# A graph layer with residual layernorm: a circular order of blocks and rounds, and one chunk before the loop of pairs

## The chip, the cores and the metric

The kernel runs on one core of a Trainium2 chip. The metric is the time of the kernel on the device in microseconds; the median of three timed runs before the change is 714.42 us (713.59 to 715.35).

## The reference

There are 100,000 nodes with 64 features (x), and 50,000 edges with 32 features each (edge_attr), a source and a destination node. The edges come sorted by destination, and destinations are drawn as 100000 * u^2 with u uniform, so they crowd at the low nodes.

```python
msg = jnp.concatenate([x[row], edge_attr], axis=1) @ W1 + b1      # 96 -> 128
agg = jax.ops.segment_sum(msg, col, num_segments=x.shape[0])
y = x + jnp.concatenate([x, agg], axis=1) @ W2 + b2               # 192 -> 64
out = (y - mean(y)) / sqrt(var(y) + 1e-5)                         # per node, over 64 features
```

## The kernel before

**Algebra.** W1 is multiplied with the part of W2 that meets agg, so an edge needs only z = [x[src], edge_attr, 1] @ wz with 64 columns. The mean over features is taken out of the weights (wz, wx, b2), and the residual is put into wx, so that what is left of the layernorm is a root and a product.

**Edges.** They are cut into chunks of 128 (392 places, CHUNKS), taken in the descending order, from the edges of the last nodes to those of node 0. Eight chunks are an edge round, 49 rounds in all (PAIRS). GpSimd gathers the rows of x for a round by eight indirect DMAs (`gather`, L381) into one of two halves of two buffers (feat), ScalarE's queue loads edge_attr beside them (L560). TensorE transposes (`turn`, L409) and multiplies with wz (`message`, L417). z is kept as three bf16 parts whose sum is the fp32 value: ScalarE makes the high part (`z_highs`, L578) and the middle (`z_mids`, L584), VectorE the rest after the high part (`z_rests`, L725) and the low part (`z_lows`, L792). All of z stays in SBUF.

**Nodes.** 1024 nodes are a block (98 of them), 256 a group (4 in a block), two blocks a unit (49 units, `unit`). For each block VectorE makes one-hots from the chunks' destinations (`one_hots`, L806) and copies z's window of these chunks (L809); TensorE multiplies one with the other into ps_y (`block_sum`, L490, 12 matmuls a group for two chunks), and adds x @ wx (L468 transposes x, L481 multiplies) and the bias (L477). ScalarE squares with a sum (L596), keeps y (L600), takes the root (L608), VectorE the reciprocal (L837) and the product (L842, for the unit before); SyncE's queue loads x and stores out.

**How many chunks.** A group of 256 nodes may have its edges in 1 to 20 chunks. The first two are always taken. If any group of a block has more (register `second`), all four groups take a second pair, in the same buffers, once TensorE has summed the first (`group_summed`). If any group still has more (`third`), each such group runs a loop over further pairs (L830 one-hots into onehot_x, L521 matmuls straight from z; one buffer for each of the pair's two chunks, given back by `hotx_used`).

**What sets the order.** At the start the kernel finds with VectorE for each group its first and last chunk (L729 to L739), makes from them the steps of each block (steps) and, for each round, how many units may have run (units: all blocks whose chunks are there, but at most AHEAD = 2.125 blocks a round), and brings both through DRAM into one row, from which the engines read registers. Loop round k of TensorE, ScalarE and VectorE does edge round k (or the steps of rounds just before it) and then the units that index k - LAG of the table adds (LAG = 2). The last indices (46 to 49 on TensorE) are unrolled copies of the unit's code behind the loop, each skipped by a branch where it has no unit. At index 49 all remaining units run.

## Time and profile before

| | us |
|---|---|
| median of the timed runs | 714.42 |
| profiled execution | 712.24 |
| its span, first to last instruction | 710.3 |
| TensorE matmul busy | 566.6 (80%) |
| VectorE busy | 519.7 (73%) |
| GpSimd busy | 398.9 (56%) |
| ScalarE busy | 397.4 (56%) |
| mean granted TensorE clock (1 is full) | 0.907 |

Busy counts instructions that compute or move; loads of registers, branches and semaphore steps are not in it, and where an engine stands idle for them the profile writes "issue". L numbers are lines of the kernel before. A row of a timeline merges like instructions: start, length, engine, line, what is written from what, how many, and in brackets the idle time just before and what ended it.

### The profile page before, as it was taken

To read this page: it belongs to the slowest core of one execution; us is meant where nothing else is said; L and a number is where in the kernel's file an instruction comes from. 1 tells how busy PE (TensorE), PEld (TensorE's weight loads), DVE (VectorE), ACT (ScalarE), POOL (GpSimd) and SP (SyncE) were. 2 spreads that over 40 slices of the span, in tenths; PEclk is the share of its full clock that TensorE was granted. 3 is DMA by queue.
4 is the path that set the end of the run, shared out by engine and by line. 5 is a ranking of instruction groups with operands and counts; after the bars stand their busy time and mean duration, and the time that the engine had idled before them with its cause. 6 is when DMAs were issued, how large, how long until landed. Compare 5 with 4: busy or idle time off the path is not lost. (4 is left out here: it accounts for less than half of the span.)

```text
span 710.3 us, 28935 instructions
## 1 busy us (share of the span) xinstructions
PE 566.6 (80%) x8370; PEld 507.2 (71%) x8371; DVE 519.7 (73%) x1820; ACT 397.4 (56%) x2012; POOL 398.9 (56%) x418
## 2 busy tenths in 40 slices
PE   1365798998888888898889888898888888873774
PEld 1355687888777877787778878787777777763653
DVE  2684677778788877778778778778888888863443
ACT  0011478777777777777777777776544445532101
POOL 5777657777757777766774777765744444000000
PEclk9955799999999999999999999999999999985555
DMA  2122345545545555545555545554433333220002
GB/s 63 33 38 38 81 123 147 136 120 132 147 117 149 127 124 138 141 122 126 142 136 136 133 120 131 139 132 114 99 83 81 81 81 96 81 59 7 2 1 60
DMA packets 168746, 71.33 MB, mean 100 GB/s; under 512 B 61570, under 2 KB 162447, under 8 KB 168720
## 3 DMA queue, kind: packets, MB, share of 16 engines
q1 hardware_dynamic: 104592, 51.74, 25.5%
q0 software_dynamic: 12544, 12.87, 9.8%
q10 hardware_dynamic: 51584, 6.41, 5.8%
q8 instruction: 13, 0.21, 0.1%
q14 instruction: 13, 0.11, 0.1%
HBM read 45.37 MB, written 25.60 MB: 100 GB/s over the span
## 5 line engine op out<-in xcount | busy, mean ns | idle before, releaser
L381 POOL DMA_INDIRECT feat<-in_x,src_idx x392 | 391.9, 1000 | 197.9 <-issue 117.7
L806 DVE TENSOR_SCALAR onehot<-node_of_col,group_base,dst_of 128x256 bf16<-128x256 bf16 x944 | 288.0, 349 | 90.8 <-issue 81.2
L490 PEld LDWEIGHTS ps_y<-z_window,onehot 128*128 128x128 bf16 x5664 | 195.1, 100 | 48.8 <-DVE z_window L809 30.2
L490 PE MATMUL ps_y<-z_window,onehot 128*128 128x64 bf16 x5664 | 213.5, 196 | 18.0 <-DVE z_window L809 14.1
L596 ACT ACTIVATE square<-ps_y 128x64 bf16<-128x64 f32 x784 | 162.1, 238 | 94.7 <-PE ps_y L481 91.9
L596 ACT ACTIVATION_READ_ACCUMULATOR square<-ps_y 128x1 f32 x784 | 159.1, 224 | 0.0
L417 PE MATMUL ps_z<-wz,feat_t 97*128 97x64 f32 x784 | 106.0, 293 | 31.5 <-DVE z_rest L725 31.4
L481 PE MATMUL ps_y<-wx,x_t 128*128 128x128 f32 x784 | 114.9, 291 | 18.5 <-ACT x_t L589 12.7
L417 PEld LDWEIGHTS ps_z<-wz,feat_t 97*128 97x128 f32 x784 | 100.3, 207 | 40.3 <-DVE z_rest L725 36.5
L809 DVE COPY z_window<-z 128x384 bf16 x472 | 121.6, 258 | 0.0
L481 PEld LDWEIGHTS ps_y<-wx,x_t 128*128 128x128 f32 x784 | 99.1, 197 | 22.3 <-ACT x_t L589 16.5
L556 ACT ACTIVATE feat_t<-ps_t 97x512 f32<-97x512 f32 x98 | 58.5, 597 | 98.2 <-PE ps_z L417 78.9
L600 ACT ACTIVATE y_sb<-ps_y 128x512 f32<-128x512 f32 x98 | 61.4, 626 | 76.6 <-DVE yout L842 76.6
L409 PE MATMUL ps_t<-ident,feat 128*97 128x128 f32 x392 | 59.7, 297 | 33.5 <-DMA feat<-in_x,src_idx 18.2
L409 PEld LDWEIGHTS ps_t<-ident,feat 128*97 128x97 f32 x392 | 48.4, 176 | 42.7 <-issue 24.6
L842 DVE TENSOR_TENSOR yout<-y_sb,rstd 128x512 f32<-128x512 f32 x100 | 64.7, 688 | 1.7
L468 PE MATMUL ps_x<-ident,xin 128*128 128x128 f32 x392 | 56.3, 291 | 8.4 <-issue 8.4
L792 DVE TENSOR_TENSOR z<-z_rest,z 128x512 f32 (+1 forms) x49 | 33.9, 692 | 38.0 <-ACT z L584 22.2
L589 ACT ACTIVATE x_t<-ps_x 128x512 f32<-128x512 f32 x98 | 53.5, 600 | 6.9 <-PE ps_x L468 6.7
L468 PEld LDWEIGHTS ps_x<-ident,xin 128*128 128x128 f32 x392 | 48.6, 156 | 9.0 <-issue 9.0
L725 DVE TENSOR_TENSOR z_rest<-ps_z,z 128x512 f32<-128x512 f32 x49 | 33.9, 691 | 13.3 <-DVE z L792 11.8
L578 ACT ACTIVATE z<-ps_z 128x512 f32 (+1 forms) x49 | 29.2, 597 | 23.7 <-issue 17.9
(113 smaller groups left out, 214.3 us busy)
## 6 DMA issues: line engine op xcount, KB each, us to landing
xin<-in_x SPq DMA_DIRECT2D x97, 256.0 KB
out<-yout SPq DMA_DIRECT2D x97, 256.0 KB
feat<-in_x,src_idx POOLq DMA_INDIRECT x392
feat<-in_edge_attr ACTq DMA_DIRECT2D x96, 64.0 KB
z<-in_src SPq DMA_DIRECT2D x1, 192.0 KB
z<-in_dst SPq DMA_DIRECT2D x1, 192.0 KB
xin<-in_x SPq DMA_DIRECT2D x1, 128.0 KB
out<-yout SPq DMA_DIRECT2D x1, 128.0 KB
```

The costliest lines, as they stand in the source:

```text
L381: nc.gpsimd.indirect_dma_start(out=feat[h][:, feat_at(k) + feat_slot(c), 0:C], out_offset=None, in_=x[:, :], in_offset=bass.IndirectOffset ...
L409: tr = nc.tensor.transpose(ps_t[h][0:F, c * P:(c + 1) * P], feat[h][:, half * CB + feat_slot(c), :], ident[:, :])
L417: mm = nc.tensor.matmul(ps_z[:, (h * CB + c) * C:(h * CB + c + 1) * C], feat_t[h][:, c * P:(c + 1) * P], wz[:, :], start=True, stop=True)
L468: tr = nc.tensor.transpose(ps_x[h][:, g * P:(g + 1) * P], xin[h][:, g, :], ident[:, :])
L481: return nc.tensor.matmul(ps_y[h][:, g * A * C:(g + 1) * A * C], x_t[h][:, g * P:(g + 1) * P], wx[:, :], start=False, stop=(g == G - 1))
L490: mm = nc.tensor.matmul(ps_y[h][:, col:col + C], onehot[h][:, g, s, a, :], z_window[h][:, g, s, part * C:(part + 1) * C], start=False, sto ...
L556: nc.scalar.activation(feat_t[h][:, :], ps_t[h][0:F, :], ACT.Copy).then_inc(feat_ready[h], 1)
L596: sq = nc.scalar.activation(square[h][:, q, :], ps_y[h][:, q * C:(q + 1) * C], ACT.Square, accum_out=sumsq[:, h, q:q + 1])
L600: nc.scalar.activation(y_sb[h][:, :, :], ps_y[h][:, :].rearrange("p (n c) -> p n c", c=C), ACT.Copy).then_inc(y_kept[h], 1)
L806: ins = nc.vector.tensor_scalar(onehot[h][:, g, s, :, :], node_of_col[:, :, :], base, dst_of[:, bass.ds(firsts[g] + (at + s), 1)], ALU.add ...
L809: nc.vector.tensor_copy(z_window[h][:, g, :, :], z[:, bass.ds(firsts[g] + at, 2), :, :].rearrange("p s q c -> p s (q c)")).then_inc(window, 1)
L842: nc.vector.tensor_tensor(yout[h][:, :, :], y_sb[h][:, :, :], rstd[:, h, :].rearrange("p (n o) -> p n o", o=1).to_broadcast([P, G * A, C]) ...
```

## The change

The edges are no longer reversed. Rounds start at round 24 (chunk 192) and go up to the end, wrap to chunk 0 and end at chunk 191 (`chunk_at`); blocks start at block 25, go up to 97, wrap to 0 and end at 24. Unit 36 holds block 97, the cut one, and block 0. Chunk numbers in the table stay plain, and `need` is brought into the circular order by a few more short steps. The last batch of edges is three chunks that end with the last edge, and destinations that stand twice are set to -1, so there is no part of a chunk to load. ScalarE's loop over rounds is split in two by four unrolled rounds around the turn (TURN = 25, rounds 23 to 26), VectorE's by one (27); SyncE's queue gets two loops, too.

The second change is in the steps. If any group of a block has more than two chunks, all groups take one chunk in the window buffers (before: two), and what is beyond three goes through the loop in pairs, ceil((n-3)/2) of them for a group with n chunks (before: ceil((n-4)/2)).

```diff
+FIRST_BLOCK = 25
+FIRST_ROUND = 24
+FIRST_CHUNK = 2 * CB * FIRST_ROUND
+CUT_UNIT = (BLOCKS - 1 - FIRST_BLOCK) // 2
+TURN = PAIRS - FIRST_ROUND
...
+        def chunk_at(k, turned=False):
+
+            if isinstance(k, int):
+                return 2 * CB * ((k + FIRST_ROUND) % PAIRS)
+            return 2 * CB * k + (FIRST_CHUNK - (CHUNKS if turned else 0))
...
-                    pair_sum(g).then_inc(group_summed, 1)
+                    window_sum(g, 2).then_inc(group_summed, 1)
                 with pe.If(second > 0):
...
-                        pair_sum(g)
+                        window_sum(g, 1)
...
-                                                                      z[:, chunk + (4 + s), part, :], start=False, stop=False)
+                                                                      z[:, chunk + (3 + s), part, :], start=False, stop=False)
...
+            with act.Fori(LAG + 2, TURN - 2) as k:
+                act_round(k)
+            for k in range(TURN - 2, TURN + 2):
+                act_round(k)
+            with act.Fori(TURN + 2, PAIRS - 1) as k:
+                act_round(k, turned=True)
...
-            nc.vector.tensor_copy(src_idx[:, 0:LAST_CHUNK + 1], ps_t[0][:, LAST_CHUNK::-1])
-            nc.vector.tensor_copy(src_idx[:, LAST_CHUNK + 1:CHUNKS], ps_t[0][:, LAST_CHUNK + 1:CHUNKS])
-            nc.vector.tensor_copy(dst_of[:, 0:LAST_CHUNK + 1], ps_t[1][:, LAST_CHUNK::-1])
-            nc.vector.tensor_copy(dst_of[:, LAST_CHUNK + 1:CHUNKS], ps_t[1][:, LAST_CHUNK + 1:CHUNKS]).then_inc(s_idx, 1)
-            dve.wait_ge(s_idx, 1)
+            nc.vector.tensor_copy(dst_of[:, :], ps_t[1][:, 0:CHUNKS]).then_inc(s_dve, 1)
+            nc.vector.tensor_copy(src_idx[:, :], ps_t[0][:, 0:CHUNKS]).then_inc(s_idx, 1)
...
+            link(nc.vector.tensor_scalar(last[:, :], last[:, :], -1.0, None, ALU.add))
             link(nc.vector.tensor_scalar(need[:, :], first[:, :], 3.0, None, ALU.add))
             link(nc.vector.tensor_tensor(need[:, :], need[:, :], last[:, :], ALU.max))
+            link(nc.vector.tensor_scalar(far_first[:, :], first[:, :], float(FIRST_CHUNK), float(CHUNKS - 1), ALU.is_lt, ALU.mult))
+            link(nc.vector.scalar_tensor_tensor(out=far_first[:, :], in0=need[:, :], scalar=float(FIRST_CHUNK),
+                                                in1=far_first[:, :], op0=ALU.is_ge, op1=ALU.mult))
+            link(nc.vector.tensor_scalar(wrapped[:, :], need[:, :], float(FIRST_CHUNK), float(CHUNKS), ALU.is_lt, ALU.mult))
+            link(nc.vector.scalar_tensor_tensor(out=need[:, :], in0=need[:, :], scalar=float(-FIRST_CHUNK),
+                                                in1=wrapped[:, :], op0=ALU.add, op1=ALU.add))
+            link(nc.vector.tensor_tensor(need[:, :], need[:, :], far_first[:, :], ALU.max))
...
-                for g in range(G):
-                    pair(g, 0, hot_ready, window_ready)
+                for g in range(G):
+                    window_of(g, 0, 2, hot_ready, window_ready)
                 with dve.If(second > 0):
                     for g in range(G):
                         dve.wait_ge(group_summed, G * b + g + 1)
-                        pair(g, 2, hot2_ready, window2_ready)
+                        window_of(g, 2, 1, hot2_ready, window2_ready)
...
-            with dve.Fori(LAG + 2, PAIRS + 1) as k:
+            with dve.Fori(LAG + 2, TURN + 2) as k:
                 dve_round(k)
+            dve_round(TURN + 2)
+            with dve.Fori(TURN + 3, PAIRS + 1) as k:
+                dve_round(k, turned=True)
```

`window_sum(g, chunks)` and `window_of(g, at, chunks, hot, window)` are `pair_sum` and `pair` with the number of chunks as an argument in place of 2. SyncE's loads and stores follow the new order; at the cut unit the load of the part of block 97 waits for the one before it.

## Rows read from the trace of the kernel before

**Rows 1.** Table of stages: the middle, and the pair loops of the last block
```profile
core 0: us, PE busy (x) PEld busy (x) DVE busy (x) ACT busy (x) POOL busy (x), PEclk, DMA share, GB/s
...
281.40:379.20 97.80, 87.28 (x1294) 79.44 (x1292) 76.80 (x262) 71.73 (x360) 71.52 (x71) 0.97 0.54 133
679.70:701.00 21.30, 14.62 (x168) 11.38 (x168) 9.20 (x28) 0.00 (x0) 0.00 (x0) 0.53 0.00 0
```
**Rows 2.** Waits of VectorE from 300 to 400 us: total, times, longest
```profile
DVE onehot L806 <- issue: 15.4, 19, 1.0
DVE z L792 <- issue: 3.2, 9, 0.4
DVE z_rest L725 <- DVE z L792: 2.0, 8, 0.3
```
**Rows 3.** Timeline of VectorE: starts of two plain rounds, and one with two units
```profile
111.74 0.69 DVE L792 TENSOR_TENSOR z<-z_rest,z 128x512 f32 x1 [0.37 <-issue]
...
122.61 0.69 DVE L792 TENSOR_TENSOR z<-z_rest,z 128x512 f32 x1 [0.36 <-issue]
...
378.88 0.24 DVE L837 RECIPROCAL rstd<-std 128x16 f32<-128x16 f32 x1
...
387.09 0.25 DVE L837 RECIPROCAL rstd<-std 128x16 f32<-128x16 f32 x1
```
**Rows 4.** Timeline of VectorE: a round whose blocks both take a second pair
```profile
503.27 0.69 DVE L792 TENSOR_TENSOR z<-z_rest,z 128x512 f32 x1 [0.35 <-issue]
...
510.01 0.59 DVE L806 TENSOR_SCALAR onehot<-node_of_col,group_base,dst_of 128x256 bf16<-128x256 bf16 x2
510.53 0.25 DVE L809 COPY z_window<-z 128x384 bf16 x1
510.70 0.59 DVE L806 TENSOR_SCALAR onehot<-node_of_col,group_base,dst_of 128x256 bf16<-128x256 bf16 x2
...
519.62 0.69 DVE L792 TENSOR_TENSOR z<-z_rest,z 128x512 f32 x1 [0.35 <-issue]
```
**Rows 5.** Timeline of VectorE: end of unit 47, and unit 48
```profile
631.19 1.29 DVE L842 TENSOR_TENSOR yout<-y_sb,rstd 128x512 f32<-128x512 f32 x2
...
654.40 0.60 DVE L806 TENSOR_SCALAR onehot<-node_of_col,group_base,dst_of 128x256 bf16<-128x256 bf16 x2 [2.01 <-issue]
...
660.17 0.60 DVE L806 TENSOR_SCALAR onehot<-node_of_col,group_base,dst_of 128x256 bf16<-128x256 bf16 x2 [2.96 <-PE ps_y L490]
...
677.48 0.26 DVE L809 COPY z_window<-z 128x384 bf16 x1
...
681.09 0.35 DVE L830 TENSOR_SCALAR onehot_x<-node_of_col,group_base,dst_of 128x256 bf16<-128x256 bf16 x1 [2.28 <-PE ps_y L521]
...
684.19 0.65 DVE L830 TENSOR_SCALAR onehot_x<-node_of_col,group_base,dst_of 128x256 bf16<-128x256 bf16 x2 [0.83 <-PE ps_y L521]
685.67 0.65 DVE L830 TENSOR_SCALAR onehot_x<-node_of_col,group_base,dst_of 128x256 bf16<-128x256 bf16 x2 [0.83 <-PE ps_y L521]
```
**Rows 6.** Timeline of TensorE: stalls in its first unit and in its last
```profile
78.38 1.05 PE L481 MATMUL ps_y<-wx,x_t 128*128 128x128 f32 x8 [2.41 <-issue]
...
83.39 2.07 PE L481 MATMUL ps_y<-wx,x_t 128*128 128x128 f32 x8 [2.35 <-issue]
...
655.27 0.87 PE L468 MATMUL ps_x<-ident,xin 128*128 128x128 f32 x3 [6.93 <-issue]
...
680.29 1.14 PE L521 MATMUL ps_y<-z,onehot_x 128*128 x12 [1.84 <-issue]
```
**Rows 7.** Groups by line: all one-hots for the windows and for the loop
```profile
L806 DVE TENSOR_SCALAR onehot<-node_of_col,group_base,dst_of 128x256 bf16<-128x256 bf16 x944 | 288.0, 349 | 90.8 <-issue 81.2 <-PE ps_y L481 6.0 <-PE ps_y L490 3.6
L830 DVE TENSOR_SCALAR onehot_x<-node_of_col,group_base,dst_of 128x256 bf16<-128x256 bf16 x38 | 12.2, 346 | 18.1 <-PE ps_y L521 16.5 <-issue 1.5
```
**Rows 8.** Timeline of GpSimd: gathers of the first rounds
```profile
74.50 1.26 POOL L381 DMA_INDIRECT feat<-in_x,src_idx  x1 [0.30 <-issue]
...
84.95 1.00 POOL L381 DMA_INDIRECT feat<-in_x,src_idx  x1 [0.30 <-issue]
...
93.83 0.97 POOL L381 DMA_INDIRECT feat<-in_x,src_idx  x1 [7.88 <-PE ps_t L409]
```

More of the change, by code:

```diff
@@ L27 @@
 CHUNKS = BATCHES * CB
-FULL_CHUNKS = E // P
-LAST_CHUNK = -(-E // P) - 1
-E_TAIL = E - FULL_CHUNKS * P
+BATCH_EDGES = CB * P
+LAST_EDGES = E - (CB - 1) * P
+TWICE = (BATCHES - 1) * BATCH_EDGES - LAST_EDGES
 A = 2
@@ L301, in store, with store_round, load_round @@
                 sp.dma_start(dst_ap, yout[h][:, :, :].rearrange("p (g a) c -> p g (a c)", g=G)).then_inc(out_stored[h], 16)
[L303 to L304 removed]
+            def store_round(k, at, cut=0):
                 for h in range(2):
[L306 removed]
+                    free_yout(k, h, cut)
                 for h in range(2):
[L308 removed]
+                    store(k, h, out_blocks[2 * k + at + h])
             for h in range(2):
                 sp.sem_inc(yout_free[h])
[L312 to L318 removed]
+            def load_round(k, at):
+                for h in range(2):
+                    load_x(k, h, x_blocks[2 * k + at + h])
+            low, high = FIRST_BLOCK, FIRST_BLOCK - BLOCKS
+            load_round(1, low)
+            load_round(2, low)
+            store_round(0, low)
+            with sp.Fori(2, CUT_UNIT - 1) as k:
+                load_round(k + 1, low)
+                store_round(k - 1, low)
+            sp.wait_ge(x_used[0], CUT_UNIT)
+            whole, cut = tail_parts(x)
+            sp.dma_start(xin[0][0:TAIL_PARTS, TAIL_GROUPS, :], cut).then_inc(x_cut_loaded, 16)
+            load_x(CUT_UNIT, 1, x_blocks[0])
+            sp.wait_ge(x_cut_loaded, 16)
+            sp.dma_start(xin[0][:, 0:TAIL_GROUPS, :], whole).then_inc(x_loaded[0], 16)
+            store_round(CUT_UNIT - 2, low)
+            load_round(CUT_UNIT + 1, high)
+            store_round(CUT_UNIT - 1, low)
+            load_round(CUT_UNIT + 2, high)
+            for h in range(2):
+                free_yout(CUT_UNIT, h)
+            sp.wait_ge(out_ready[0], CUT_UNIT + 2)
             whole, cut = tail_parts(out)
@@ L322, in _ @@
             sp.dma_start(cut, yt[0:TAIL_PARTS, TAIL_GROUPS, :]).then_inc(out_stored[0], 16)
-            store(0, 1, out_block(1))
-            with sp.Fori(2, PAIRS - 1) as k:
-                top = sp.snap(BLOCKS - 2 * k)
-                for h in range(2):
-                    load_x(k + 1, h, x_full[top - (3 + h)])
-                store_round(k - 1, top + 1)
-            store_round(PAIRS - 2)
-            store_round(PAIRS - 1)
+            store(CUT_UNIT, 1, out_blocks[0])
+            with sp.Fori(CUT_UNIT + 2, PAIRS - 1) as k:
+                load_round(k + 1, high)
+                store_round(k - 1, high, cut=1)
+            store_round(PAIRS - 2, high, cut=1)
+            store_round(PAIRS - 1, high, cut=1)
             sp.wait_ge(out_stored[0], 16 * (PAIRS + 1))
@@ L482, in dense, with window_sum @@
                                             wx[:, :], start=False, stop=(g == G - 1))
-                def pair_sum(g):
-                    for s in range(2):
+                def window_sum(g, chunks):
+                    for s in range(chunks):
                         for a in range(A):
@@ L621, in _ @@
                 act.sem_inc(squared[h])
-            act.wait_ge(s_clear, 8)
-            load_ea_first()
-            load_ea(0, 1)
-            act.wait_ge(s_const, 13)
+            act.wait_ge(s_clear, 7)
+            for h in range(2):
+                load_ea(0, h)
+            act.wait_ge(s_const, 14)
             nc.scalar.activation(std_eps[:, :], eps[:, :], ACT.Sqrt)
@@ L801, in one_hots, with window_of @@
                 dve.wait_ge(hots_used[h], k + 1)
-                def pair(g, at, hot, window):
+                def window_of(g, at, chunks, hot, window):
                     base = group_base[:, bass.ds(b * G + g, 1)]
-                    for s in range(2):
+                    for s in range(chunks):
                         ins = nc.vector.tensor_scalar(onehot[h][:, g, s, :, :], node_of_col[:, :, :], base,
@@ L826, in one_hots @@
                                     turn_no = dve.snap(pairs_done)
-                                    chunk = nc.s_assert_within(dve.snap(firsts[g] + 2 * n), 0, CHUNKS - 6, skip_runtime_bounds_check_because="the table of steps ends every range before the last chunk")
+                                    chunk = nc.s_assert_within(dve.snap(firsts[g] + 2 * n), 0, CHUNKS - 5, skip_runtime_bounds_check_because="the table of steps ends every range before the last chunk")
                                     for s in range(2):
```

172 lines of the change are left out of this document (76 added, 96 removed).

## The prediction

> **What bounds the kernel now.** I read the table of stages first: in the long middle TensorE is busy 87.28 of 97.80 us and VectorE 76.80 [rows 1], which reads like a TensorE bound. The waits of VectorE in that stage say otherwise: from 300 to 400 us it waited for "issue" (its own sequencer: loops and register loads) and for a short step behind itself, and for no other engine [rows 2]. So its own chain of instructions sets the pace. The timeline of VectorE prices that chain: a round (eight chunks of edges, one unit of two blocks) starts at 111.74 and the next at 122.61, 10.87 us; where a round runs two units, reciprocals stand 387.09 - 378.88 = 8.2 us apart [rows 3]. So a unit costs 8.2 us of VectorE and the bare round 2.66. The rounds of blocks with a second pair take 519.62 - 503.27 = 16.35 us [rows 4], 5.5 more than a plain round: per block 4 groups, each 0.68 (two one-hots 0.52, one copy 0.17, by the starts 510.01, 510.53, 510.70), 2.74 per block. The same sum from 122.61 us (loop round 8, five units done) gives 40 x 2.66 + 43 x 8.2 + 18 x 2.74 = 508.3, so 630.9 for the end of unit 47; the trace has 631.19 + 1.29 [rows 5]. The account holds to 1 us.
>
> Behind it lies the tail. VectorE ends unit 47 at 632.5 and starts the one-hots of unit 48 at 654.40, 22 us later: the last three edge rounds go through all engines with no unit beside them, and TensorE waits 6.93 us for issue before its next x transpose [rows 6]. Unit 48 (blocks 1 and 0) then takes until the end at 710.3.
>
> **Counts.** The trace fixes those of before: 944 one-hots are 392 x 2 + 20 x 8, so 20 blocks take the second pair, and 38 one-hots of L830 are 19 pairs in the loop [rows 7]. From the reference's dst, sorted into chunks of 128, I get the same 20 and 19 (1, 4 and 14 in blocks 2, 1, 0), and so trust it for after: 21 blocks take the third chunk (97, 0 to 18 and 20), and 31 pairs are in the loop (18, 5, 4, 2, 1, 1 in blocks 0 to 5). The table of units for each round comes from the same data. Before: 2, 1, 1, 1, 1 ... from index 2 on, 48 units by index 45, the last one at index 49. After: 0, 1, 1, 2, 1, 1, 1, 2 for indices 2 to 9 (9 units either way by then), one a round to index 37 (39 units), then 7 units over indices 38 to 48 and three (46, 47, 48) at index 49; of those three only one block takes a third chunk.
>
> **Part 1, one chunk in place of a pair.** Of the 2.74 us a block, one one-hot (0.26) stays of each two. The copy of 128x192 has no row. It lies between the 0.17 of 128x384 and half of that, 0.09 [rows 4]. I take the middle, 0.13: 4 x 0.39 = 1.56 a block, 21 blocks 32.8 us against 20 x 2.74 = 54.8. Gain 22.0 (20 to 23.5). TensorE's 456 fewer window matmuls (960 before, 21 x 24 after) save nothing of their own there, since it waits for VectorE's windows in those rounds.
>
> **Part 2, more pairs in the loop.** Block 0 before: last window copy 677.48 + 0.25, the second pair's one-hot at 681.09, so 3.36 us to get in, most of it TensorE loading its registers (1.84 issue [rows 6]) while VectorE waits; then 685.67 - 684.19 = 1.48 a pair, one-hots and matmuls taking turns through one buffer each [rows 5]. On VectorE before: block 0 22.5, block 1 7.3, block 2 0.7, together 30.5. After: 4 blocks x 3.36 = 13.4, 25 further pairs x 1.48 = 37.0, and blocks 4 and 5 with one pair and no wait 1.3 each: 53.0. Loss 22.5. The 1.48 has the 12 matmuls at the half clock (granted 0.53 there [rows 1]), 1.04 us of it. At the full clock they would take half, so 1.48 - 0.26 (half of one buffer's six) = about 1.2: lower end 22.5 - 7 = 15. Upper end, 1.8 a pair with the switches of groups (block 1's 7.3 over 4): 30.
>
> **Part 3, the circular order at the start.** Before, index 2 has two units at once. After, the first block needs 14 chunks, so index 2 has none, and VectorE idles behind the gathers: POOL needs 84.95 - 74.50 = 10.45 us for eight [rows 8], and before TensorE has units these set the pace. Gathers of round 5 end at 75.8, its transposes at about 77, those of rounds 6 and 7 follow about 10.4 apart. The first unit on TensorE costs twice a warm one (two stalls of 2.4 for issue, and the half clock; before it ended at 83.39 + 2.07 [rows 6]): it ends at about 96. Then unit 1 and the two of index 5 follow, and VectorE starts round 8 at about 120 with 4 units done; before it was 122.61 with 5. Loss 8.2 - 2.6 = 5.6 (3 to 9). The ten or so extra short steps in making the tables (0.2 us each) lie beside the wait for those gathers: nothing; uncovered they would be 2. Dropping the reversed copies saves VectorE four column copies, also hidden.
>
> **Part 4, the circular order at the end.** Idle of VectorE before: 21.9 between 632.5 and 654.4, less three rounds of its own work (8.0), 13.9; and 2.96 for TensorE at 660.17 [rows 5]. After, units 44 and 45 lie between the last rounds. What is left: ScalarE makes the middle part of round 47 only after the high part of round 48, which waits for TensorE's message behind unit 44 (3.7 us of VectorE idle), and about 1.2 for one-hot buffers in the last units. Gain 16.9 - 4.9 = 12.0 (6 to 15). From the last one-hot to the end it is 10.1 before and as much after: dense matmuls, squares, root, product, store.
>
> TensorE's first pass through unrolled units is the doubt here. The tail has one copy of the unit's code for each of indices 46, 48 and 49, where before only that of 49 ran. Twice 2.4 per copy [rows 6] lies partly in the 1 to 2 us a unit by which TensorE is ahead. The Trainium skill, page "Runtime: NRT & Kernel Launch", section "Instruction fetch mechanics", says that a taken branch to a page outside the current window must fetch before going on. If each skipped section and skipped copy stalled so with nothing to hide it, the eight such jumps of the tail at 2.4 would be 19 us, and the gain of this part gone. The rows show such stalls in the first unit and in the tail, and none at the like places of the loop once it is warm, which agrees.
>
> **Part 5, what the middle pays.** (a) The pair loops now stand before warm rounds. In the pair loops before, the clock was at its lower level nearly throughout (0.53 [rows 1]), after TensorE had worked in bursts of 1.04 in 1.48 us. After it, TensorE starts blocks 1 to 6 at half speed, where its 9.7 us a round (87.28/97.80 of 10.87) goes towards 19 against VectorE's 14 to 30: 5 us until it has caught up (0 to 12). (b) ScalarE runs four rounds and VectorE one from unrolled copies near the turn, with new loops behind: VectorE's first window in such a copy was late by 1 us (2.01 issue [rows 5] against 1.0 at most in the loop [rows 2]); with the tail 4 us in all (0 to 8). Skewed x loads at the cut block, two DMAs one behind the other, lie beside a unit of 8 us: nothing. Edge, x and output transfers keep their number and sizes.
>
> **Sum.** -22.0 + 22.5 + 5.6 - 12.0 + 5 + 4 = +3.1 us on the span of 710.3: 713.4. The profiled execution took 712.24 (1.9 around its span), the median of the timed ones is 714.42, 2.2 above it. So 714.42 + 3.1 = 717.5.
>
> **Rivals.** *A, the pair loop and the cold code are cheap.* In mid-stream the clock stays at its upper level (it is 0.97 in the middle [rows 1]), a pair costs 1.2, nobody meets cold code: -22.0 + 15.5 + 5.6 - 14 + 0 + 1 = -14, so 700. For it: VectorE alone waited only for issue at its first entry into the loop. Against: in a pair loop TensorE has at most 0.53 of 1.2 us to do, less than where the clock fell before. In part (3 or more us kept of these) the kernel is already faster, about 709.
> *B, TensorE becomes the bound.* The clock stays down through units 36 to 40 and the three cold copies of the tail are exposed: +3.1 + 7 + 9 = +19, so 733 (727 to 736 with less or more of it). For it: the half clock after 679.7 us never recovered while pair loops ran. Against: plain units fill TensorE densely, and hold the clock at 0.97 in the middle [rows 1].
> *C, the rounds without a unit are bound by the gathers.* Indices 38, 40, 43 and 47 run no unit; at 10.45 us of POOL instead of 2.66 four of them would cost 31, so 748. POOL runs up to two rounds ahead and waited 7.88 us for TensorE [rows 8]; the units between last 14 us and more, so I count it as small.
> *D, the new order of blocks and rounds is made but the tail keeps its wait*, since three units still have to follow the last chunk: +3.1 + 12 = 729, inside B's place.
>
> **Chances.** The near cancellation 0.48 (its own range 712 to 724), A 0.26, B and D 0.22, C 0.04. Within 0.3% (2.1 us, about what can be told from no change) is the lower third of the first case: 0.17. Faster: A and the lowest edge of the first, 0.33. Slower: 0.50. Range 701 to 732: it holds nearly all of A and the nearer half of B.
>
> **What would show it.** L806 x868 one-hots, L809's line x476 copies, L830's line x62, TensorE's window matmuls 4704 + 504 = 5208. Rounds of about 14 us with third chunks; block 0's stretch of VectorE near 500 us, 25 to 30 us long; no idle of 8 us in VectorE's last 80 us; loop round 8 at 120. I am wrong if the pair loops run at the full clock, if TensorE's waits for VectorE vanish in the second half, or if POOL gathers until the end.

## The result: slower by 4.15%

The changed kernel took 743.62 us median of 4 runs (742.46 to 745.17), the kernel before beside it 714.00 (713.09 to 715.35): a ratio of 1.0415, 95% interval [1.0388, 1.0441]. I had forecast 717.5, from 701 to 732. The profiled execution took 742.46, with a span of 740.6 against 710.3.

The page's groups by line (columns: line, engine, operation, tiles, count | busy us, mean ns of one | idle before and what ended it), which answer to [rows 7], and the stages that answer to [rows 1]:

```profile
L831 DVE TENSOR_SCALAR onehot<-node_of_col,group_base,dst_of 128x256 bf16<-128x256 bf16 x868 | 268.0, 350 | 107.0 <-issue 89.6
...
L509 PE MATMUL ps_y<-z_window,onehot 128*128 128x64 bf16 x5208 | 205.0, 198 | 21.8 <-DVE z_window L834 17.7
...
L834 DVE COPY z_window<-z 128x384 bf16 (+1 forms) x476 | 117.9, 248 | 0.0
```

```profile
core 0: us, PE busy (x) PEld busy (x) DVE busy (x) ACT busy (x) POOL busy (x), PEclk, DMA share, GB/s
281.40:379.20 97.80, 87.02 (x1316) 78.15 (x1314) 76.77 (x261) 72.57 (x369) 74.30 (x72) 1.00 0.53 132
476.00:502.00 26.00, 17.75 (x204) 13.76 (x204) 11.01 (x34) 0.00 (x0) 0.00 (x0) 0.56 0.00 0
```

The counts are those forecast (868, 476, 5208), so the kernel does what it says. The middle is as before, 76.77 against 76.80 us of VectorE. The pair loops of block 0 now run in mid-stream, from 476 on, at the same low clock (0.56 against 0.53).

To see where the 30 us came from, I followed VectorE's starts of a round (the first tensor_tensor on z of each loop index; the list of starts is worked out from its timeline). Both kernels have finished 36 units when they start round 37: before at 454.3, after at 461.6, 7.3 later. From there to the end it is 256.0 and 279.0, 23.0 more. Rounds 37 to 50, us each:

```
round   37    38    39    40    41    42    43    44    45    46    47    48    49    50
before 10.9  10.8  13.6  13.6  16.3  17.7  16.4  16.3  16.4  29.6  16.8  10.1   6.7   2.1
after  42.5  30.8  22.3   8.2  22.2   6.0  18.0  16.2   6.0  18.3  14.6  16.3   6.7  14.0
```

Rounds 40, 42 and 45 after run no unit. I had counted such a round at VectorE's own 2.66 us. VectorE's timeline of the kernel after, for the first two of them and the block behind the first (start, length, ..., idle before and what ended it):

```profile
558.09 0.69 DVE L734 TENSOR_TENSOR z_rest<-ps_z,z 128x512 f32<-128x512 f32 x1 [0.26 <-DVE z L817]
565.32 0.69 DVE L817 TENSOR_TENSOR z<-z_rest,z 128x512 f32 x1 [6.54 <-ACT z L596]
...
573.61 0.35 DVE L831 TENSOR_SCALAR onehot<-node_of_col,group_base,dst_of 128x256 bf16<-128x256 bf16 x1 [3.12 <-PE ps_y L509]
...
593.49 0.69 DVE L817 TENSOR_TENSOR z<-z_rest,z 128x512 f32 x1 [4.32 <-ACT z L596]
```

VectorE stands 6.54 and 4.32 us for ScalarE's middle part of z, and, between the two, 3.12 us in round 41's first block, ahead of its third chunk, for TensorE's sums of the first two chunks, since that chunk goes through the same window buffer. VectorE's waits from round 37 to the end, after:

```profile
DVE onehot L831 <- issue: 31.7, 29, 2.8
DVE onehot_x L855 <- PE ps_y L540: 24.5, 25, 2.2
DVE z L817 <- ACT z L596: 20.2, 4, 6.5
DVE onehot L831 <- PE ps_y L509: 13.6, 16, 3.2
```

and before, from its round 37 to its end:

```profile
DVE onehot L806 <- issue: 23.6, 27, 2.0
DVE onehot_x L830 <- PE ps_y L521: 16.5, 16, 2.3
DVE z L792 <- ACT z L584: 14.1, 3, 8.4
...
DVE onehot L806 <- PE ps_y L490: 3.6, 2, 3.0
```

The wait for ScalarE, which my part 4 took to be mostly gone, grew from 14.1 to 20.2; that for TensorE's window sums went from 3.6 to 13.6; the pair loops' from 16.5 to 24.5.

### The profile page after: what moved, and what is told of

Read it like the earlier page. It is cut to its first block and busy times, and to the rows that moved or that the text cites. A ratio compares the mean times of both kernels' runs of the same rounds, so it can differ in the third digit from the quotient of the medians.

```text
span 740.6 us, 27987 instructions
## 1 busy us (share of the span) xinstructions
PE 591.2 (80%) x8058; PEld 524.3 (71%) x8059; DVE 507.3 (69%) x1777; ACT 399.4 (54%) x2012; POOL 399.0 (54%) x418
## 3 DMA queue, kind: packets, MB, share of 16 engines
q1 hardware_dynamic: 104592, 51.74, 24.5%
## 5 line engine op out<-in xcount | busy, mean ns | idle before, releaser
L403 POOL DMA_INDIRECT feat<-in_x,src_idx x392 | 392.9, 1002 | 249.4 <-PE ps_t L428 122.9
L831 DVE TENSOR_SCALAR onehot<-node_of_col,group_base,dst_of 128x256 bf16<-128x256 bf16 x868 | 268.0, 350 | 107.0 <-issue 89.6
L509 PEld LDWEIGHTS ps_y<-z_window,onehot 128*128 128x128 bf16 x5208 | 185.9, 101 | 56.2 <-DVE z_window L834 32.8
L509 PE MATMUL ps_y<-z_window,onehot 128*128 128x64 bf16 x5208 | 205.0, 198 | 21.8 <-DVE z_window L834 17.7
L436 PE MATMUL ps_z<-wz,feat_t 97*128 97x64 f32 x784 | 112.5, 305 | 26.6 <-DVE z_rest L734 26.4
L436 PEld LDWEIGHTS ps_z<-wz,feat_t 97*128 97x128 f32 x784 | 106.9, 219 | 37.2 <-DVE z_rest L734 33.5
L834 DVE COPY z_window<-z 128x384 bf16 (+1 forms) x476 | 117.9, 248 | 0.0
L428 PE MATMUL ps_t<-ident,feat 128*97 128x128 f32 x392 | 65.6, 316 | 39.3 <-DMA feat<-in_x,src_idx 17.4
L428 PEld LDWEIGHTS ps_t<-ident,feat 128*97 128x97 f32 x392 | 54.0, 192 | 48.2 <-issue 22.8
L487 PE MATMUL ps_x<-ident,xin 128*128 128x128 f32 x392 | 58.8, 300 | 1.7 <-issue 1.7
L540 PE MATMUL ps_y<-z,onehot_x 128*128 x372 | 32.1, 227 | 24.4 <-DVE onehot_x L855 18.3
L540 PEld LDWEIGHTS ps_y<-z,onehot_x 128*128 128x128 bf16 x372 | 24.6, 112 | 31.8 <-issue 28.8
## 6 DMA issues: line engine op xcount, KB each, us to landing
xin<-in_x SPq DMA_DIRECT2D x97, 256.0 KB
out<-yout SPq DMA_DIRECT2D x97, 256.0 KB
```

The costliest lines, as they stand in the source:

```text
L403: nc.gpsimd.indirect_dma_start(out=feat[h][:, feat_at(k) + c, 0:C], out_offset=None, in_=x[:, :], in_offset=bass.IndirectOffsetOnAxis(ap=s ...
L428: tr = nc.tensor.transpose(ps_t[h][0:F, c * P:(c + 1) * P], feat[h][:, half * CB + c, :], ident[:, :])
L436: mm = nc.tensor.matmul(ps_z[:, (h * CB + c) * C:(h * CB + c + 1) * C], feat_t[h][:, c * P:(c + 1) * P], wz[:, :], start=True, stop=True)
L487: tr = nc.tensor.transpose(ps_x[h][:, g * P:(g + 1) * P], xin[h][:, g, :], ident[:, :])
L509: mm = nc.tensor.matmul(ps_y[h][:, col:col + C], onehot[h][:, g, s, a, :], z_window[h][:, g, s, part * C:(part + 1) * C], start=False, sto ...
L831: ins = nc.vector.tensor_scalar(onehot[h][:, g, s, :, :], node_of_col[:, :, :], base, dst_of[:, bass.ds(firsts[g] + (at + s), 1)], ALU.add ...
```

## Experiments

In every kernel below but desc_even and desc_even2 the first unit's number of a round passes through a max with zero (the register is never negative, so this changes no work). The kernels ran in five groups (the expectations say "call" for a group), each on one chip and beside the kernel before. In groups 1 and 4 that took 712.97 and 712.38 us, in groups 2, 3 and 5 it took 1067.88, 1068.70 and 1070.08 (the slow groups below). So times compare within a group only; where I set kernels of two groups side by side below, I take each less the kernel before of its own group.

**Group 1: the two parts of the change apart.** The control circ_c is the changed kernel with that max. circ_two has the circular order with the second pair of before; desc_one has the order of before with one chunk in place of the second pair (both edits in short, side by side):

```
 circ_two (against after)                 desc_one (against before)
-window_of(g, 2, 1, ...)                 -for s in range(2): onehot of 2 + s
+window_of(g, 2, 2, ...)                 +for s in range(1)
-chunks beyond three in the loop         -chunks beyond four in the loop (19 pairs)
+chunks beyond four (19 pairs)           +chunks beyond three (31 pairs)
```

> The changed kernel with one more register step per round on each engine: the number of units already done goes through a max with 0 before it starts the loop of units. Nothing else differs. It is the control for the kernels beside it, which all carry this step. One step of 0.1 us or less in about 45 rounds, beside other work: 743 to 747, against 743.6 of the changed kernel.

> The circular order with the steps of before: a second pair for all groups of a block (21 blocks, 20 plus the one with block 97), and only then pairs in the loop, 19 as before in place of 31. Theory E: the two kinds of steps cost the same within 3 us (2.74 against 1.56 us a block is +22, twelve pairs at 1.48 and three entries fewer is -22), so 740 to 747. Theory P: the pair loops in mid-stream are what costs; with twelve fewer, and none in blocks 3 to 5, it is 10 us or more faster than the control, 733 or less. Theory O (the single one-hot catches up with TensorE: VectorE waited 13.6 us in 16 waits for the sum of the first pair before it wrote the third chunk): these waits go, 730 to 736.

> The descending order of before with the second change alone: one chunk for all groups of 20 blocks, then 31 pairs in the loop in place of 19. My sum for this part was -22.0 and +22.5: 712 to 717. Theories P and O, by which this part carries the loss: 725 or more. Theory E, by which the order carries it: within 4 us of 714.

circ_c: 745.79, ratio 1.0445 [1.0386, 1.0505]. circ_two: 738.07, 1.0354 [1.0313, 1.0394]. desc_one: 719.09, 1.0103 [1.0055, 1.0152]. The chunk costs 6.1 us alone (desc_one less before) and 7.7 in the circular order. The order costs 25.1 (circ_two less before) or 26.7 (circ_c less desc_one). The two add up, and four fifths of the loss is the order. Neither of these two times lies in a range that I had written down. 738.07 stands midway between theory O's 736 and theory E's 740; but VectorE's waits for TensorE's sums, which O said would go, are 16.0 us in its trace. 719.09 is 1 to 2 us above the upper ends of my sum and of theory E, and 6 below P and O. Rounds with two third-chunk blocks last 14.7 in desc_one against 16.35 in [rows 4]: 0.8 a block saved, where I had 1.18. One-hot and copy of the one chunk are 0.38 us apart by their starts, as I had it (0.39); the 0.7 us by which a round is longer than my 13.98 lies between the blocks, as issue: 1.06 and 1.43 us ahead of the two blocks of round 41, where before had 0.98 and 0.75 in the round of [rows 4]. Over the whole stretch from round 37 VectorE's waits for issue before a window are 30.5 us in desc_one and 23.6 in before, 6.9 more, which is about the chunk's price of 6.1. What VectorE's sequencer does in them isn't shown.

**Group 1: one unit for each index.** circ_even is circ_c with another table of units, so that no index is without one from 3 to 48:

```
-AHEAD = 2.125
+AHEAD = 2.0
-nc.gpsimd.iota(round_no[:, :], pattern=[[0, 1]], base=0,
+nc.gpsimd.iota(round_no[:, :], pattern=[[0, 1]], base=-2,
```

> The changed kernel with another table of units: at most 2 * (k - 2) blocks by index k, in place of 2.125 * k. By the reference's dst this gives one unit for every index from 3 to 48 and three at index 49, so no round without a unit (before: indices 38, 40, 43, 47) and none with two. Theory E (rounds without a unit): in loop rounds 40, 42 and 45 the chain transpose, feat_t, message, high, rest, middle, low passes the engines with nothing beside it (8.2, 6.0 and 6.0 us where VectorE has 2.66 of work), and the unit behind starts with TensorE late (16 to 22 us where the account has 14 to 15.3). Then 15 to 25 us come back: 720 to 729. Theory P (the pair loops and TensorE at its half clock behind them): the table changes neither, within 4 us of the control.

It took 727.66 us (720.55 to 731.79), ratio 1.0176 [1.0110, 1.0241], 18.1 less than circ_c and within theory E's 720 to 729; its runs spread over 11 us, so the 18.1 is good to some 6 us either way. VectorE's waits from its round 37 to the end (in the execution of 731.79) have no row for ScalarE's z at all:

```profile
...
DVE onehot L839 <- PE ps_y L517: 14.4, 22, 5.0
...
DVE z L825 <- issue: 4.4, 13, 0.4
DVE rstd L870 <- ACT std L628: 4.2, 1, 4.2
DVE z_rest L742 <- DVE z L825: 3.4, 13, 0.3
```

So the rounds without a unit are a large part of the loss. The waits for TensorE's sums stay (14.4, in 22 waits). 11.2 of them lie between 550 and 602 us, in the two rounds with the last four pairs, in which the granted clock was 0.63 and 0.61; that the clock makes them is likely and not tested.

**Group 4: both orders without any pair loop.** circ_nopairs3 and desc_one_nopairs3 leave the chunks beyond the third out of the sums, by a table that says zero pairs; the same two had run in groups 2 and 3 as circ_nopairs, circ_nopairs2, desc_one_nopairs and desc_one_nopairs2. circ_c2 is the control again.

```
-link(nc.vector.reduce_sum(far_first[:, 1:2], pairs_f[:, :], axis=AX.X))
+link(nc.vector.tensor_scalar(far_first[:, 1:2], block_need[:, :], 0.0, None, ALU.mult))
```

> The circular control without any pair loop (the chunks beyond the third are left out of the sums). Theory 1 (the 31 passes and the entries to their blocks cost 1.5 us and 3.5 us): 45 us less than circ_c2 of this call. Theory 2 (0.73 us a pass, as in my sum): 25 us less.

> The descending order with one chunk beyond two, without any pair loop (the chunks beyond the third are left out). Against circ_nopairs3 it differs in the order alone. Theory 1 (the rounds without a unit cost 6 us each): 12 to 20 us faster than circ_nopairs3 where VectorE bounds the plain rounds, and equal where TensorE does. Theory 2 (the order costs only through its pair loops): within 5 us in both cases.

> The control (the changed kernel, with the first unit's number held at zero or more) beside the kernels of this call. If the chip is like that of the first call: a ratio of 1.044 as there. If it is like that of the second and third, where each plain round is bound by TensorE: theory 1 (the order's rounds without a unit and the pair loops are longer than VectorE's own work whatever TensorE does) a ratio of 1.01 to 1.03, theory 2 (there the order costs nothing, since the loop's rounds are TensorE's) 0.99 to 1.00.

circ_c2: 745.31, ratio 1.0449 [1.0405, 1.0494], as in group 1. circ_nopairs3: 686.32 (682.51 to 691.22), 0.9627 [0.9561, 0.9693]. desc_one_nopairs3: 659.70 (658.82 to 660.59), 0.9258 [0.9222, 0.9293]. Two prices follow. The loops cost 59.0 us in the circular order (circ_c2 less circ_nopairs3), and 58.8 in that of before (desc_one of group 1 and desc_one_nopairs3, each less its own before), so where they stand makes no difference. And the order costs 26.6 us with no loop in either kernel, the same as with them. Both are more than theory 1 had (45 and 12 to 20), and far from theory 2 (25 and under 5). The two times, 686.32 and 659.70, lie in the ranges that I had set from the rounds of the traces for circ_nopairs and desc_one_nopairs (678 to 687, 658 to 666). The order's price has nothing to do with where it puts the loops.

What the price is shows in VectorE's waits from round 37 to the end, circ_nopairs3 first:

```profile
DVE onehot L839 <- issue: 30.7, 28, 2.6
DVE z L825 <- ACT z L604: 18.0, 4, 5.0
DVE onehot L839 <- PE ps_y L517: 12.4, 11, 3.1
DVE z L825 <- issue: 3.4, 10, 0.4
...
DVE rstd L870 <- ACT std L628: 2.7, 1, 2.7
```

and desc_one_nopairs3:

```profile
DVE onehot L812 <- issue: 30.4, 26, 2.1
DVE z L798 <- ACT z L592: 9.6, 2, 5.0
DVE z L798 <- issue: 5.8, 13, 1.9
DVE rstd L843 <- ACT std L616: 4.0, 1, 4.0
...
DVE onehot L812 <- PE ps_y L498: 1.6, 4, 1.1
```

That is 8.4 more for ScalarE's z and 10.8 more for TensorE's sums, 15.8 in all with the smaller rows; from round 37 to the end the two kernels differ by 222.0 - 203.5 = 18.5. The other 10.1 of their spans (685.5 and 656.9) has been lost by round 37. The descending order has rounds without a unit too, 48, 49 and 50 (6.2, 6.7 and 3.3 us), so the 18.5 is the difference of two kernels that both pay for such rounds. The chain inside round 40 of circ_nopairs3, over three engines (VectorE's, TensorE's and ScalarE's timelines):

```profile
509.06 0.69 DVE L825 TENSOR_TENSOR z<-z_rest,z 128x512 f32 x1 [0.34 <-issue]
510.00 0.69 DVE L742 TENSOR_TENSOR z_rest<-ps_z,z 128x512 f32<-128x512 f32 x1 [0.26 <-DVE z L825]
515.02 0.69 DVE L825 TENSOR_TENSOR z<-z_rest,z 128x512 f32 x1 [4.32 <-ACT z L604]
...
523.31 0.34 DVE L839 TENSOR_SCALAR onehot<-node_of_col,group_base,dst_of 128x256 bf16<-128x256 bf16 x1 [3.04 <-PE ps_y L517]
```

```profile
510.75 2.00 PE L444 MATMUL ps_z<-wz,feat_t 97*128 97x64 f32 x16 [0.93 <-DVE z_rest L742]
514.37 2.45 PE L436 MATMUL ps_t<-ident,feat 128*97 128x128 f32 x8 [1.62 <-DMA feat<-in_edge_attr]
516.71 3.68 PE L444 MATMUL ps_z<-wz,feat_t 97*128 97x64 f32 x16
...
522.31 2.69 PE L517 MATMUL ps_y<-z_window,onehot 128*128 128x64 bf16 x66
```

```profile
511.95 0.60 ACT L583 ACTIVATE feat_t<-ps_t 97x512 f32<-97x512 f32 x1 [0.77 <-PE ps_z L444]
...
513.62 0.60 ACT L598 ACTIVATE z<-ps_z 128x512 f32 x1 [0.18 <-issue]
514.12 0.62 ACT L604 ACTIVATE z<-z_rest 128x512 f32 x1
```

Read it in this order: VectorE's rest (510.00) frees the one PSUM tile of messages; TensorE then multiplies for 2.00 us; ScalarE, which has waited for those matmuls to copy the transposed features, writes the high part at 513.62 and the middle part at 514.12; VectorE's low part follows at 515.02 and the round is over, 5.96 us after 509.06, when it began. No engine works through it, they take turns (of the 5 us from 509 on TensorE is busy 2.82, VectorE 1.38, and ScalarE 3.75, 2.2 of that still for the unit before). Beside a unit of 8 us this chain is hidden; alone it is the round. One link of it is the program's own: ScalarE's middle part needs only VectorE's rest, which was there at 510.69, but `act_round` has it behind the high part of the next round, which needs TensorE's products. No run moved it ahead.

Then TensorE waits 1.62 for edge_attr, and its transposes and products take 2.45 and 3.68 us where those just before took 1.09 and 2.00: the granted clock was 1.00 from 509 to 512 and 0.50 from 513 to 523, and fell behind the wait of 0.93 and within that of 1.62. So its first window sums end past 523, and VectorE's third chunk waits 3.04. That is read from the timeline: no run took the edge_attr wait or the low clock away here, so how they share the 3.04 isn't shown. The round behind lasts 17.8 instead of 14.7. An empty round costs 6.0 - 2.66 + 3.1 = 6.4 us above my count, three of them 19, about what circ_even gave back (18.1).

In groups 2 and 3, where TensorE bounds the plain rounds (in circ_nopairs it is busy 105.88 and waits 53.2 for issue of the 160 us from 300 on), these two kernels took 1016.31 and 1018.45, then 1018.67 and 1016.64 us: equal. Taken for an answer on the order, that would have been theory 2's; group 4 shows that it held only for such runs.

> The control circ_c without the loop of pairs: the register that lets a block into it is 0 for all blocks, so all that lies beyond a group's third chunk (blocks 0 to 5) is left out of the sum. All else runs. My account had 53 us for the 31 pairs, which would give 692. From the trace of the changed kernel the rounds 37, 38, 39 and 41 took 117.8 us, where a round with two third chunks and no pair took 14.6 (round 47), so 59 goes there, and TensorE no longer falls to its lower clock: rounds 40, 42 and 43 lose another 5. 678 to 687.

> The same work left out of desc_one (descending order, one chunk, 31 pairs there). Rounds 46 and 47 had 32.8 and 28.2 us and should have 26.7 and 14.7, and the last unit loses 28.5 for block 0 and 9.3 for block 1: 57 us, 719 to 662 (658 to 666). If the pairs were dearer in mid-stream than in the tail (theory P), less than 50 comes back here and over 60 in the circular order; if the order's loss lies in the rounds without a unit and in the tail (theory E), the two differences agree within 5 us.

> The circular control without any pair loop (the chunks beyond the third of every group are left out of the sums; the number of pairs is written as zero), with the kernels of this call on one chip. Theory 1 (the 31 passes of the pair loops cost what the trace after shows, 1.48 us a pass at half TensorE clock and about 3.5 us of VectorE for each block that enters a loop at all, with waits for TensorE's group sums behind them): about 45 us less than the control's 745.8, a ratio to before of 0.98, and the rounds 37, 38, 39 last about 17, 17 and 15 instead of 42.5, 30.8 and 22.3. Theory 2 (the loops cost VectorE's own 0.73 us a pass, as my sum has it, and the loss lies in the order): about 25 us less, a ratio of 1.01. Both: the rounds without a unit (40, 42, 45) stay at 6 us.

> The descending order with one chunk beyond two, without any pair loop (the chunks beyond the third are left out). Against circ_nopairs2 it differs in the order alone, with no pair in either. Theory 1 (the order's own price is that of its three rounds without a unit, 6 us each where a unit's round has room for one): 12 to 20 us faster than circ_nopairs2, a ratio to before of 0.95 to 0.96. Theory 2 (the order costs only by where it puts the pair loops, at half clock): within 5 us of circ_nopairs2.

**Groups 3 and 5: the edge_attr load issued first.** circ_ea (and circ_ea3) moves ScalarE's load of the next batch ahead of its copies.

```
 for h in range(2):
-    keep_feat(k, h)
-    load_ea(k + 1, h, turned)
+    act.wait_ge(ea_loaded[h], 16 * (k + 1))
+    load_ea(k + 1, h, turned)
+for h in range(2):
+    keep_feat(k, h)
```

> The circular control with ScalarE's load of the next edge_attr batch issued ahead of the copies of the transposed features, not behind them. Theory 1 (a round without a unit lasts 6 us because TensorE waits in it for a load that ScalarE has issued late, 1.5 us a half): the rounds 40, 42 and 45 last about 4.5 instead of 6.0 to 8.2, and the time is 5 us less than the control's, a ratio of 1.037. Theory 2 (such a round is a chain of transposes, copies, products and rests over three engines, and the load is beside it): within 1.5 us of the control, a ratio of 1.043 to 1.047.

> The circular control with ScalarE's loads of the next edge_attr batch issued ahead of its copies of the transposed features. Theory 1 (a round without a unit is 6 us long for that late load): rounds 40, 42 and 45 last about 4.5 us, a ratio of 1.037. Theory 2 (the chain of transposes, copies, products and rests is what it lasts): 1.043 to 1.047.

1077.08 (1.0077 [1.0040, 1.0113]) and 1077.24 (1.0061 [1.0038, 1.0085]), in the slow groups, without the control circ_c beside them, so the time says little. The empty rounds say more: 8.7, 7.4 and 7.6 us in circ_ea3, against 7.5, 7.6 and 6.5 in circ_busy3 of the same group, which has the loads where they were (and fillers in its pair loops, so it is no clean control). They got no shorter, which speaks for theory 2, the load beside the chain. Where the kernel before takes 712 us it wasn't measured, so whether an earlier load would save some of the 3 us behind an empty round stays open.

**Groups 2, 3 and 5: filler matmuls at the loops.** circ_busy (circ_busy2, circ_busy3) keeps TensorE at work to hold its clock.

```
 with pe.If(third > 0):
+    fill(12)
 ...
+        fill(2)
         pe.wait_ge(hotx_ready[s], done)
```

> The control circ_c with matmuls that compute nothing needed, into a PSUM bank of their own, where TensorE stands idle about the pair loops: 12 of 128x256 bf16 before a block's registers are loaded and 2 before each chunk of a pair. If TensorE's lower clock is what makes the pair loops and the rounds behind them slow, the granted clock goes from about 0.7 to near 1 from 465 to 600 us, a pair from 1.48 to 1.2, and VectorE's waits for TensorE's sums (3 to 5 us in the rounds behind) go: 725 to 735. If the entry and the pair are bound by register loads and the round trip, the filling only adds to it: 745 to 755.

> The circular control with filler matmuls on TensorE ahead of each block's pair loop (12) and in each pass (2), to a PSUM tile that nothing reads. Theory 1 (the half clock behind TensorE's waits makes a pass of a loop 1.48 us instead of VectorE's own 0.73): the granted clock in the first stretch of loops rises from half to full, a pass lasts 0.9 to 1.1, and the time is 8 to 12 us less than the control's, a ratio of 1.03. Theory 2 (a pass is a chain between VectorE and TensorE, its waits and issue gaps, whatever the clock): a pass lasts 1.4 or more, and the time is that of the control or up to 5 us over it, a ratio of 1.045 to 1.05.

> The circular control with filler matmuls on TensorE ahead of each block's pair loop (12) and in each pass (2). Theory 1 (half clock makes a pass long): a pass in the first block with loops lasts 0.9 to 1.1 us instead of 1.48, and the time is 8 to 15 us less than the control's 745.3, a ratio of 1.025 to 1.035. Theory 2 (a pass is a chain of VectorE, its issue gaps and TensorE's answer): 1.4 us a pass or more, a ratio of 1.044 to 1.055.

1070.58, 1072.77 and 1073.12 us, ratios 1.0040 [1.0022, 1.0059], 1.0036 [1.0009, 1.0063] and 1.0025 [1.0007, 1.0044]. The stretch of block 0's loops, circ_busy2 and then circ_ea3, whose TensorE has no fillers (columns as above):

```profile
745.00:775.00 30.00, 25.57 (x348) 19.25 (x347) 15.00 (x57) 1.75 (x16) 0.00 (x0) 0.91 0.00 0
```

```profile
760.00:775.00 15.00, 10.63 (x122) 8.31 (x122) 6.58 (x21) 0.00 (x0) 0.00 (x0) 0.50 0.00 0
```

One pass with fillers, VectorE and TensorE:

```profile
766.15 0.65 DVE L871 TENSOR_SCALAR onehot_x<-node_of_col,group_base,dst_of 128x256 bf16<-128x256 bf16 x2 [0.79 <-PE ps_y L556]
767.59 0.65 DVE L871 TENSOR_SCALAR onehot_x<-node_of_col,group_base,dst_of 128x256 bf16<-128x256 bf16 x2 [0.79 <-PE ps_y L556]
```

```profile
766.54 0.39 PE L524 MATMUL ps_idle<-node_of_col 128*128 128x256 bf16 x2 [0.24 <-issue]
766.77 0.58 PE L556 MATMUL ps_y<-z,onehot_x 128*128 x6
767.18 0.38 PE L524 MATMUL ps_idle<-node_of_col 128*128 128x256 bf16 x2
767.40 0.34 PE L556 MATMUL ps_y<-z,onehot_x 128*128 x6
```

The clock rose from 0.50 to 0.91, and a pass still takes 1.44 us against 1.48: my forecast of 0.9 to 1.1 failed. But the four fillers of a pass lie in TensorE's row between the real matmuls (0.22 us each two, by the starts) and take back what the clock gave, so this doesn't tell what a pass would last at the full clock alone. It stays open. In the times of group 4 the fillers weren't measured.

**Groups 2 and 4: one unit for each index in the order of before.** desc_even and desc_even2 are the kernel before with AHEAD = 2.0, nothing else.

> The kernel before (descending order, second pairs) with at most 2.0 blocks a round in place of 2.125, so that units 44 to 47 run at indices 45 to 48 beside the last edge rounds, where before there was none. Before, VectorE had 8 us of work in the 21.9 between its last two units. Theory E: most of the 13.9 comes back, 700 to 706. If a tail without units costs nothing (the last unit sets the end anyway): 712 to 715.

> The kernel before with 2.0 instead of 2.125 indices for a block, so that each index has one unit: no round of two units. Theory 1 (two units in a round cost no more than two rounds, and what counts is the number of units left behind the last index): 0 to 6 us faster, a ratio of 0.992 to 1.0. Theory 2 (one unit fewer in the tail is paid by one more far-window unit in the loop at the same price): 0.998 to 1.002. On the chip of the second call it had 0.9936.

desc_even2: 704.84 us (704.35 to 705.46), ratio 0.9884 [0.9847, 0.9922]; desc_even, in a slow group, 1060.49, 0.9936 [0.9918, 0.9954]. It is the fastest complete kernel here, 7.5 us under the one before. That is within what I had given theory E for desc_even (700 to 706) and more than either theory had for desc_even2. Its rounds 48 to 50 last 17.9, 18.7 and 16.5 us where before had 10.1, 6.7 and 2.1 with no unit, and the row of VectorE's wait for ScalarE's z, 14.1 us before, is gone from its waits:

```profile
DVE onehot L814 <- issue: 30.2, 29, 2.9
...
DVE z L800 <- issue: 4.4, 12, 0.4
DVE onehot L814 <- PE ps_y L498: 4.1, 3, 2.0
DVE rstd L845 <- ACT std L616: 3.9, 1, 3.9
DVE z_rest L733 <- DVE z L800: 3.1, 12, 0.3
...
```

Half of the 14.1 is not gained: the waits for issue before a window are 30.2 where before had 23.6. The gap that the circular order was to fill, my part 4, is filled by one constant: a unit less early, so that one is left for each of the last rounds.

The evened tables also tell how much of the order's price the empty rounds are. circ_even is 14.7 above before; without 6.9 for the chunk that is 7.8, and desc_even2 is 7.5 below. So with no empty round in either, the circular order still costs about 15 us of its 25 to 27 (give or take the 6 of circ_even): some 11 net are the empty rounds, and 7 to 10 are already lost at round 37.

## Why the prediction was wrong

Step by step, with what I had beside what was measured:

- *The start (part 3), +5.6.* Round 8 started at 120.5 (I had about 120), and by round 37 the kernel was 7.3 late. The reason was right and the size near, at the upper end of my 3 to 9 or above it: circ_nopairs3 and desc_one_nopairs3 differ there by 10.1, circ_c and desc_one by 10.7.
- *The chunk (parts 1 and 2), -22.0 + 22.5 = +0.5.* Measured 6.1 and 7.7. That the two nearly cancel is right in the main, and both terms were a little off to the same side: about 0.8 to 1.0 saved a block (rounds 39 to 45 of desc_one 98.6 us against 110.3, twelve blocks) instead of 1.18, which is 4 to 8 us on twenty; and the loops after 59.0 us in all, by leaving them out, where I had 53.0 and 5 of clock behind them.
- *The middle, +5 for the clock.* It lies in those 59.0: outside rounds 37 to 39, which hold 30 of the 31 passes, circ_c2 is 2.2 us longer than circ_nopairs3 in round 40, and 4.4 in round 41 with the last pass. Of the right size.
- *The cold copies, +4.* From round 37 on VectorE's waits for issue before a window are 30.7 us in the circular order and 30.4 in that of before, without loops; with loops 31.3 against 30.5 (circ_c, desc_one), and with second pairs 25.7 against 23.6 (circ_two, before). So 0.3 to 2.1 us are left of this term. My eight jumps at 2.4 us, 19 in all, didn't come either: in the tail TensorE waits for issue 6.9 us in circ_nopairs3 (from 611 on) and 8.9 in desc_one_nopairs3 (from 600 on). The rule that I weighed them by is that of the Trainium skill (page "Runtime: NRT & Kernel Launch", section "Instruction fetch mechanics"); these traces have waits for issue that would agree with it, but no more of them in the circular order.
- *The tail and the circular order at the end (part 4), -12.0.* This is the step that failed. I wrote "Gain 16.9 - 4.9 = 12.0". From round 37 on the order costs 18.5 instead of gaining. I had seen in [rows 5] and [rows 6] that the last three edge rounds "go through all engines with no unit beside them", and took that for a matter of the tail. It is the matter of any round without a unit, and the new table has three of them in the middle (indices 38, 40 and 43), as I had listed, and one at 47 that keeps a wait of 5.0 in the tail. I counted each at 2.66 us, VectorE's work beside a unit; they last 6.0 to 8.2, with 3 more for the round behind. I even had the mechanism: for round 47 I wrote that ScalarE makes the middle part only after the high part of the next round, and gave it 3.7 us, once; for rounds 40, 42 and 45 I put it at nothing.

How much of the miss this is can be added up. My prices for the stretch from round 37 on (14 rounds at 2.66, 13 units at 8.2, the third chunks at 1.56 a block, the waits I named and 10.1 to the end) give 202.0 us for desc_one_nopairs3, with 20 blocks and the 16.9 of waits read from the tail of before, and 191.6 for circ_nopairs3, with 21 blocks and 4.9. They took 203.5 and 222.0. So the account holds for the descending order and is 30.4 short for the circular one. Of that, 10.0 are the three empty rounds, 12.0 the rounds behind them, 8.5 the other seven rounds with third chunks (rounds 38, 44 and 48 last 16.2 to 16.3 where I had 13.98); the fourth empty round, 49, is 4.0 above my count, within the waits that I had allowed. My check of the account in the prediction couldn't show it: all 40 rounds that it summed had a unit (and it held to 1.6 us, 630.9 against 631.19 + 1.29, not to 1).

Rival C had the right place and nearly the right time, 748, for the wrong cause: it said the gathers of such rounds bind. They don't; GpSimd waits for TensorE (122.9 us over the kernel, 83.8 of them from round 37 on), and the feature transposes of round 40's chain wait for edge_attr and PSUM, not for a gather. I set its chance at 0.04 because I argued only against its cause. That its 748 comes near 743.6 is luck in part: it had 31 us for four such rounds and nothing for the rounds behind them. Rival B (733) and D (729: the tail keeps its wait) were nearer than the forecast; D is true as far as it goes, the 5.0 at index 47. Of what would show it, "no idle of 8 us in VectorE's last 80 us" came true (5.0 at most) while the idle had moved ahead of that stretch: a sign that looked at one place for a wait that could move.

The sum with measured terms: 7.3 to 10.7 (start) + 18.5 (order from round 37) + 6.9 (chunk, middle of 6.1 and 7.7) = 32.7 to 36.1. circ_c2 is 32.9 above before, circ_c 32.8; the changed kernel without the max was 29.6 above, in other runs.

## What to carry to other kernels

A price read from a pipelined round (here 2.66 us, a round with a unit less the unit) holds only where the neighbour that hides the chain is there. Before counting a stage alone at its bounding engine's work, walk its chain over all engines once, and look in the trace for a place where it already runs alone: in the tail of before a bare round (49) takes 6.7 us, which was that price:

```profile
642.90 0.69 DVE L792 TENSOR_TENSOR z<-z_rest,z 128x512 f32 x1 [8.41 <-ACT z L584]
...
649.59 0.69 DVE L792 TENSOR_TENSOR z<-z_rest,z 128x512 bf16<-128x512 f32 x1 [5.04 <-ACT z L584]
```

And when work is reordered, look at the table that couples the streams for entries of zero: spreading the units evenly gave back 18 us in one order and gained 7.5 in the other, more than I had hoped to get from the reordering (12.0 at the end less 5.6 at the start).

## What the runs showed of the hardware

One and the same kernel was 50% slower in some groups of runs. desc_even took 1060.49 us and desc_even2, the same text, 704.84; the kernel before 1068 to 1070 in three groups and 712 in two. Within a group the kernel before repeats within 1%, but it need not be a matter of the chip: the numbers on record are chips 9, 14, 0, 2 and 2, and groups 4 (712.38) and 5 (1070.08) have the same one. TensorE's waits from 300 to 460 us, in desc_even and then in desc_even2:

```profile
PE ps_y L498 <- issue: 55.3, 68, 1.9
```

```profile
PE ps_z L425 <- DVE z_rest L733: 9.9, 13, 0.9
```

In the slow one TensorE's stream of window matmuls stops 68 times in 160 us, for 0.8 us on average, for nothing that the profile shows (issue), and rounds 34 to 39 last 17.5 to 20 us instead of 10.9. VectorE's one-hots take the same time in both (349 and 345 ns each). The profile's rows of instruction DMA are the same in both (16 and 13 packets), so what holds the sequencer isn't shown; it stays open. A change that matters where VectorE is the bound (the order, 26.6 us) is nothing there (1016.31 against 1018.45), and a comparison of times across two groups would have been wrong by 350 us.
